# The heads' pass of a fused attention kernel in another order: third queries' split in the preceding pass, no filler products

## The reference, cut to what matters

```python
k1 = jnp.concatenate([kn, jnp.broadcast_to(kr, (B, N_HEAD, T, ROPE))], -1)
o1 = _attn(q, k1, v1, causal[None, None])            # all earlier tokens ("far")
ks = jnp.concatenate([ks[..., :NOPE], _rope(ks[..., NOPE:], cos, sin)], -1)
o2 = _attn(q, ks, vs)                                # 256 selected tokens
kw = jnp.concatenate([kw[..., :NOPE], _rope(kw[..., NOPE:], cos, sin)], -1)
o3 = _attn(q, kw, vw, winmask[None, None])           # a window of 64 tokens
o = g[:, 0] * o1 + g[:, 1] * o2 + g[:, 2] * o3
return o.transpose(0, 2, 1, 3).reshape(B, T, N_HEAD * VDIM) @ Wproj
```

## Time and profile before

| | |
|---|---|
| median of 3 runs | 2601.32 us (2599.31 to 2602.56) |
| the profiled execution, its own time | 2596.9 us |
| its span | 2594.7 us |
| PE busy | 2348.2 us, 91% |
| DVE busy | 1813.2 us, 70% |
| ACT busy | 1409.9 us, 54% |
| POOL busy | 1261.8 us, 49% |
| begin of the last pass of the heads | 2322.93 |

### The profile page before, as it was taken

One profiled execution on the slowest core, in us unless ns is written; L12 is line 12 of the kernel. 1 busy time (PEld: TensorE's weight loads), 2 busy tenths in 40 slices (PEclk: granted clock), 3 DMA queues, 4 the chain that ended last, 5 costly groups with the idle time before them and its releaser, 6 DMA issues. The chain is left out here.

```text
span 2594.7 us, 51630 instructions
## 1 busy us (share of the span) xinstructions
PE 2348.2 (91%) x16877; PEld 1703.1 (66%) x16877; DVE 1813.2 (70%) x3640; ACT 1409.9 (54%) x2487; POOL 1261.8 (49%) x965
## 2 busy tenths in 40 slices
...
DMA packets 82190, 128.15 MB, mean 49 GB/s; under 512 B 15824, under 2 KB 58241, under 8 KB 81729
## 3 DMA queue, kind: packets, MB, share of 16 engines
q1 hardware_dynamic: 77616, 119.47, 18.3%
...
q10 hardware_dynamic: 1472, 0.24, 0.1%
...
## 5 line engine op out<-in xcount | busy, mean ns | idle before, releaser
L2662 ACT ACTIVATE a_PT<-PS 128x512 f32<-128x512 f32 (+1 forms) x1104 | 584.0, 565 | 362.2 <-PE PS L2518 243.7
L2371 POOL TENSOR_TENSOR a_KT<-a_PT 128x256 f32<-128x256 f32 (+2 forms) x175 | 349.5, 2008 | 452.9 <-ACT a_PT L2662 444.4
L2731 DVE TENSOR_REDUCE a_NM<-PS 128x2 fp32r<-128x512 f32 (+2 forms) x512 | 290.9, 612 | 129.6 <-PE PS L2462 69.3
L2371 POOL TENSOR_TENSOR a_KT<-a_KT,a_PT 128x1024 f32<-128x1024 f32 (+1 forms) x122 | 370.9, 3040 | 8.5
L2512 PE MATMUL PS<-a_QH,a_K 128*128 128x512 f32 (+3 forms) x768 | 291.9, 390 | 1.1 <-ACT a_PT L2662 1.0
L2743 DVE TENSOR_REDUCE a_MX<-PS 128x1 f32<-128x512 f32 (+3 forms) x432 | 265.9, 665 | 32.7 <-PE PS L2477 18.1
L2512 PE MATMUL PS<-a_QH,a_KSW 128*128 128x192 f32 (+3 forms) x832 | 263.9, 338 | 12.1 <-DVE a_NM L2731 10.5
L2477 PE MATMUL PS<-a_K,a_QH 128*128 128x512 f32 (+3 forms) x768 | 252.4, 404 | 9.3 <-DVE a_K L2718 7.9
L2513 PE MATMUL PS<-a_QL,a_K1B 76*128 76x512 f32 (+3 forms) x768 | 259.3, 348 | 0.0
L2462 PE MATMUL PS<-a_KSW,a_QH 128*128 128x256 f32 (+2 forms) x1024 | 197.1, 304 | 4.0 <-DVE a_QL L2715 4.0
L2462 PEld LDWEIGHTS PS<-a_KSW,a_QH 128*128 128x128 f32 x1024 | 162.6, 192 | 49.3 <-DVE a_NM L2731 19.5
...
## 6 DMA issues: line engine op xcount, KB each, us to landing
...
```

Of the source, the lines that this page charges most:

```text
L2371: nc.gpsimd.tensor_tensor(total, one_in, other_in, ALU.add).then_inc(s["added"], 1)
L2662: nc.scalar.activation(PT[:, to:to + width], turning(key)[:, 0:width], ACT.Exp).then_inc(s["taken"], 1)
L2731: nc.vector.tensor_reduce(NM[:, i, DH:].rearrange("p (h x) -> p h x", x=3)[:, h:h + 2, x], ring(key)[:, 0:2 * w].rearrange("p (h n) -> p h ...
```

## The change

The list is another one, from its first row to its last, with the same steps; and the nine unread products are gone. The tiles, the rings' rules, the instructions of each step and all other stages stay as they are. Of the table the first and the last row are shown, and the function:

```diff
 ORDER = """
-wk tr.q2 tr.q3 split.tr.q2 split.tr.q3
+wk tr.q3
...
-+score.3.0 +rope.w3 +v.vw.1 +rope.q2 ysum.5 +v.vs.0 +tr.w3 +split.tr.w3 +a.q3 +rot.q3 +double.w3 project.5 +value.0.0 +value.1.1 +value.2.2 +add.0 +add.1 +value.3.3 +add.2 +add.3 +add.4 +add.5 +add.6 +sum.0 +rope.q3 +norm.0
++score.3.0 +v.vw.1 +a.q3 +split.tr.w3 +tr.q2 +value.0.0 ysum.5 +rot.q3 project.5 +value.1.1 +add.0 +add.1 +add.2 +split.tr.q2 +value.2.2 +add.3 +add.4 +value.3.3 +add.5 +double.w3 +add.6 +sum.0 +rope.q3 +norm.0
...
                     after(pe, q, at, bank_free(key, q))
-                    if i == 4 and n == 0:
-                        keep_clock(9, bank)
                     after(pe, q, at, *(("reduced", ("split", "tr", g)) for g in made))
```

More of the change, by code:

```diff
@@ L1997 @@
 ORDER = """
-wk tr.q2 tr.q3 split.tr.q2 split.tr.q3
+wk tr.q3
 score.4.0
-score.4.1 v.v1.0 near.4.0
+score.4.1 v.v1.0 split.tr.q3 near.4.0
 score.4.2
 score.4.3
-score.5.0 +load.next near.4.1 near.4.2 near.4.3
-score.5.1 near.5.0
+score.5.0 near.4.1 +load.next near.4.2 near.4.3
+score.5.1 v.v1.1 near.5.0 near.5.1
 score.5.2
-score.5.3 near.5.1 near.5.2 v.v1.1 near.5.3 near.6.0 value.4.4 near.6.1 near.6.2 near.6.3 turn.0.2 near.7.0 value.5.5 add.7 near.7.1 near.7.2 k1.0 near.7.3
-score.6.0 split.k1.0 k1.1 sum.1 norm.1 turn.0.3 k1.2 split.k1.1 split.k1.2
@@ L2008 @@
-score.6.1 k1.3 split.k1.3
-score.7.0
+score.5.3 near.5.2 near.5.3 near.6.0 value.4.4 near.6.1 near.6.2 near.6.3 turn.0.2 near.7.0 value.5.5 near.7.1 add.7 near.7.2 k1.0 near.7.3 sum.1
+score.6.0 split.k1.0 turn.0.3 k1.1 norm.1
+score.6.1 k1.2 k1.3
+score.7.0 split.k1.1 split.k1.2 split.k1.3 value.6.6
 score.7.1
-score.8.0 far.0.0 value.6.6 value.7.7 value.8.8 far.1.0 far.1.1
-score.9.0 far.2.0 far.2.1 far.2.2 turn.1.0 far.2.3
-score.9.1 far.3.0 far.3.1 ysum.1 far.3.2
+score.8.0 far.0.0 far.1.0
@@ L2014 @@
+score.9.0 far.1.1 value.7.7 far.2.0 value.8.8 far.2.1 turn.1.0 far.2.2
+score.9.1 far.2.3 far.3.0 far.3.1 far.3.2
 score.10.0 far.3.3
-score.11.0 far.4.0 far.4.1
+score.11.0 far.4.0 ysum.1 far.4.1
 score.11.1
[L2017 to L2022, removed]
@@ L2037 @@
[L2037 to L2041, removed]
+score.11.2 add.8 far.4.2
+score.11.3 add.9 far.4.3 far.4.4 +load.own far.5.0 value.9.9 value.10.10 far.5.1 far.5.2 join.4 value.11.11 far.5.3 far.5.4 add.10 add.11 add.12 add.13 add.14
+score.12.0 turn.1.1 far.5.5
+score.12.1 double.k0 far.6.0
+score.12.2 far.6.1 far.6.2
+score.12.3 add.15
+score.13.0 far.6.3
@@ new lines @@
+score.13.1 far.6.4 far.6.5 sum.2 value.12.12 +a.s norm.2
+score.13.2
+score.13.3 +rot.s far.6.6 far.6.7 add.16 sum.3 norm.3 join.5 value.13.13
+score.14.0 +a.w0
+score.14.1 +rot.w0
+score.14.2 far.7.0
+score.14.3 far.7.1 join.6 far.7.2
+score.15.0 far.7.3 turn.1.2
+score.15.1 +rope.s far.7.4 far.7.5
+score.16.0 far.7.6 +rope.w0 +tr.s far.7.7 add.17 +a.w1 join.7 add.18 turn.1.3 value.14.14 add.19 +split.tr.s +tr.w0 +rot.w1 add.20 value.15.15 +a.q0
+score.17.0
+score.17.1 ysum.3
+score.17.2
+score.17.3
@@ L2042 @@
+score.18.0
+score.18.1 +rope.w1 +rot.q0 +split.tr.w0 +tr.w1
+score.18.2 value.16.16
+score.18.3 +v.vw.0 +rope.q0 +split.tr.w1 add.21 +tr.q0 sum.4 norm.4 +split.tr.q0 ysum.4 value.17.17 +a.q1 +a.w2 value.18.18 double.k1
 score.19.0
-score.19.1 double.k1
-score.19.2 +rot.q1 +near.0.0 +near.0.1
-score.19.3
+score.19.1 +rot.w2
+score.19.2 +rot.q1 +near.0.0
+score.19.3 +near.0.1
 score.20.0
[L2047 to L2050, removed]
+score.20.1 +near.0.2
```

39 lines of the change are left out of this document (15 added, 24 removed).

## The result

The changed kernel takes 2618.95 us (median of 4 runs, 2615.99 to 2624.38), the one before in the same session 2601.94 (2599.31 to 2602.58): 1.0066 of it, with an interval of 1.0048 to 1.0084. It is slower by 17 us, where I had forecast 20 us less. The time lies outside my range.

What follows compares the result with a forecast made beforehand. PE's list of work was taken to bound each pass; the terms -2.9 + 0.45 - 2.2 + 0.85 + 1.8 + 2.2 - 1.3 gave -1.1 us a pass, about 20 us in all, so 2581 us, range 2550 to 2604.

Steps and rivals of the forecast that it cites:

- The begin: Start of a pass: `score.5.1` at 5.65 us instead of 8.55, 2.9 less; `tr.q2` adds 0.45 in the preceding pass.
- The clock: PE's clock without the unread filler products: stays at 1.00, so the sum takes nothing for it.
- rival D: Clock falls once a pass behind the 1.8 us wait ahead of `sum.0`: +0.3 a pass, 2606 us; chance 0.05.
- The middle: `sum.1` moved before `score.6.0`; three waits in the pass go, -2.2 us, a new one of `score.6.1` comes, +0.85.
- The end: `rot.q2` and `rope.q2` delay POOL's additions behind `sum.5`, so PE waits 1.8 us ahead of `sum.0`.
- The ring: Banks for PE's products: `tr.q2` last and `tr.q3` first share bank 0, so `tr.q3` waits for `split.tr.q2`.
- rival E: Slower if `split.tr.q2` ends late and holds `tr.q3` in the shared bank: +1.0 a pass, 2617 us; chance 0.09.
- The borders: Value steps alone between other products: 0.27 us a border pair, ten more runs, +2.2 us a pass.
- The spreading: Near, far and score products alternating more evenly: 1.3 of 2.3 us of weight-load waits saved a pass.
- rival A: Bigger gain from a smaller end wait or cheaper borders: 2.9 us a pass, 2554 us; chance 0.28.

Runs made afterwards that it cites:

- e2: The kernel before with only the new begin: `tr.q2` and its split in the preceding pass, no unread products; 2577.15 us, 0.9896 of the kernel before.
- e1: The kernel before without its nine unread products, order unchanged; 2623.9 us, 1.0086 of the kernel before.
- e5: The changed kernel with its value steps put back into runs, nothing else moved; 2599.68 us, 0.9994 of the kernel before.
- e7: The kernel before with only the stretch from behind `near.7.3` to `score.11.1` in the new order; 2592.94 us, 0.9957 of the kernel before.
- e6: The changed kernel with `rot.q2` and `rope.q2` back ahead of `norm.5` and `ysum.5`; 2603.14 us, 0.9998 of the kernel before.
- e10: The kernel before, unread products kept, with seven value steps moved out of their runs; 2631.45 us, 1.0105 of the kernel before.
- e11: The kernel before with `score.13.1` to `score.20.3` in the new order but value runs kept; 2611.08 us, 1.0024 of the kernel before.
- e12: The kernel before with the stretch from behind `score.20.3` to `turn.0.0` in the new order; 2607.35 us, 1.0021 of the kernel before.

## Why the prediction was wrong

**The begin, -2.9 + 0.45.** Right: 5.69 where 5.65 was forecast, -2.86; `tr.q2` 0.38 in e2. ACT was next, as said, with a wait of 0.45 of `score.4.3`.

**The clock, 0, and rival D.** Right in the changed kernel: 1.00 in all passes, with a wait of 1.5 and no unread products. My reason, that a wait of 1.64 left the clock alone, was weaker than I gave it out: e1 shows that without the products behind it this wait costs the clock. Had the new wait been the 1.8 that I forecast, D would have come in part: e5 has it, and loses the clock in three passes of fifteen, 0.7 us each. So that it did not come is partly luck.

**The middle.** Right in sum. The waits of 0.65, 0.49 and 0.66 went; the new one of `score.6.1` was 0.43 and not 0.85. These are DVE's transpose and the score that waited for it.

```profile
1242.31 0.72 DVE L2756 STREAM_TRANSPOSE a_RT<-PS 128x512 f32<-128x512 f32 x1
```

```profile
1243.08 0.36 PE L2510 MATMUL PS<-a_QH,a_KSW 128*128 128x192 f32 x1 [0.43 <-DVE a_RT L2756]
```

The transpose ended 3.47 us behind the start of `near.7.3` (1239.56), as counted (3.4); it was PE that came later, busy until 3.09 where I had 2.65. e7 shows -0.70 for this stretch alone.

**The end, +1.8.** Right in mechanism, 1.5 in size; e6 gives 1.14 of it back.

**The ring, rival E.** The place was right and the sign open: e2 shows its wait, 0.91 us, but in the changed kernel POOL's wait hides it.

**The borders, +2.2.** The price of 0.27 is right where PE is the bound (e10). In the changed kernel e5 gives 1.18 for nine of the ten, for those in the middle were hidden.

**The spreading, -1.3.** This is the step that failed. I read the 2.3 us of weight loads waiting for maxima as time that PE lost at full rings, and gave 1.3 of it to a more even list. First, it was no lost time. These are PE's `value.5` and the weight load behind it in the sixth pass of the kernel before and, apart, a row of the waits of its weight loads that had nothing to wait for ("issue").

```profile
1231.24 1.07 PE L2538 MATMUL PS<-a_PT,a_VS 128*32 128x512 f32 x8
...
1232.24 0.53 PEld L2462 LDWEIGHTS PS<-a_KSW,a_QH 128*128 128x128 f32 x4 [0.84 <-DVE a_NM L2731]
```

```profile
PEld PS L2512 <- issue: 23.5, 28, 0.8
```

Each of the two rows is two waits a pass, 0.84 + 0.38 and 0.84 + 0.24. The 0.84 stands behind a value step, whose weights are loaded in its first 0.16 us; then the loads pause while PE works on its products, and PE has no gap. The same 0.84 stands in the last row, behind `value.21` and behind `sum.5`, where no maximum was waited for at all. Second, the new list did not take these waits away. These are the two rows in the changed kernel.

```profile
PEld PS L2460 <- DVE a_NM L2729: 28.7, 42, 0.8
...
PEld PS L2475 <- DVE a_MX L2741: 14.5, 28, 0.8
```

That is 3.1 us a pass in place of 2.3. Third, another order has a price of its own: +0.50 in e11 for one stretch, +0.46 between `score.11.1` and `score.13.1` by the table, +0.46 in e12 with three parted values in it. A part of it is just what the spreading was to take away, a product held by a maximum on DVE: `a.w1` in e11, with the same four lengths in the changed kernel, and there `a.w3` too, whose weight load waits 0.27 for a near maximum that ends at 1319.35; it starts at 1319.40. Take the measured terms together: -2.86 + 0.38 - 0.70 - 0.66 (the wait of `sum.5`) + 1.5 + 1.18 = -1.16. The pass became +1.27, so 2.4 us are left for spreading and neighbours where -1.3 was written: off by 3.7 us a pass, 56 us in all, more than the whole miss of 38. Of the 2.4, the three pieces named hold at most 1.4. The rest, in the last 20 us of the pass and around, no run separates; by the starts of the steps 0.2 of it stands at `tr.q2` (0.59 to the next step), 0.2 at `value.0.0` and `project.5`, and 0.2 where `score.0.1` parts `value.24` from `sum.5`.

One slip in rival A moves no term: half way between gains of 1.1 and 4.0 is 2.55, not 2.9, so its time is 2559 and not 2554.
